# A gated cross-attention and spiking-FFN layer: attention's rows kept in PSUM, high halves read in place, and a new order on every engine

## What is computed

```python
def _mlstm_cell(q, k, v, igate_w, igate_b, fgate_w, fgate_b, ln_scale):
    ...
    log_f = jax.nn.log_sigmoid(fg)
    cs = jnp.cumsum(log_f, axis=1)
    ...
    log_D = log_fg_mat + ig[:, None, :]
    max_log_D = jnp.max(log_D, axis=-1, keepdims=True)
    D_mat = jnp.exp(log_D - max_log_D)
    qk = jnp.einsum('hsd,htd->hst', qh, kh) / np.sqrt(DH)
    C = qk * D_mat
    normalizer = jnp.maximum(jnp.abs(C.sum(axis=-1, keepdims=True)), jnp.exp(-max_log_D))
    h = jnp.einsum('hst,htd->hsd', C / (normalizer + EPS), vh)
    ...
    return (h - mu) / jnp.sqrt(var + LN_EPS) * ln_scale

def _L0_ffn_ref(x, W_fc, W_proj):
    h = jnp.square(jax.nn.relu(jnp.einsum('bsd,fd->bsf', x, W_fc)))
    y = jnp.einsum('bsf,df->bsd', h, W_proj)
    def step(mem, _):                      # 5 steps
        reset = spike_fn(mem - THRESHOLD)
        mem_new = BETA * mem + y - reset * THRESHOLD
        return (mem_new, spike_fn(mem_new - THRESHOLD))
    ...
    return jnp.sum(spks, axis=0) / NUM_STEPS

x = x + jnp.tanh(g_xattn[0]) * _L0_xattn_ref(_layernorm(x), ctx_1024, ctx_1024, ...)
x = x + jnp.tanh(g_ffn[0]) * _L0_ffn_ref(_layernorm(x), L0_ffn_W_fc, L0_ffn_W_proj)
```

## Time and profile before

| | us |
|---|---|
| time, median of 3 runs | 738.58 |
| lowest, highest | 737.99, 739.53 |
| the profiled execution's own time | 738.68 |
| its span | 736.9 |
| PE busy | 631.4 |
| PEld busy | 528.3 |
| DVE busy | 597.5 |
| ACT busy | 466.7 |
| POOL busy | 396.5 |

### The profile page before, as it was taken

How to read it: one execution, slowest core, us unless ns; L and a number is a source line. 1 busy time by engine, 2 the same in 40 slices (tenths; PEclk the granted TensorE clock), 3 DMA queues, 4 the chain that set the end, 5 groups by cost and what they waited for, 6 DMA issues and landing times. The chain is left out here.

```text
span 736.9 us, 17412 instructions
## 1 busy us (share of the span) xinstructions
PE 631.4 (86%) x6064; PEld 528.3 (72%) x6064; DVE 597.5 (81%) x1314; ACT 466.7 (63%) x1020; POOL 396.5 (54%) x427
## 2 busy tenths in 40 slices
PE   0254686889999989998999989998999999999985
PEld 0144675768787778877888778877887887787875
DVE  4577668889799979998799979997999889878543
ACT  4366665578577847676667747684778756764431
POOL 5346636656584656576466657575556645642000
PEclk9998789989999999999999999999999999999998
DMA  6946513396155724564266606672455444100000
GB/s 209 156 104 138 124 45 84 88 166 142 30 133 110 138 61 102 117 132 102 73 104 136 154 19 132 124 146 63 103 117 89 88 74 86 63 1 29 30 30 28
DMA packets 73174, 71.31 MB, mean 97 GB/s; under 512 B 8704, under 2 KB 68736, under 8 KB 73088
## 3 DMA queue, kind: packets, MB, share of 16 engines
q1 hardware_dynamic: 71968, 70.02, 44.8%
q10 hardware_dynamic: 1120, 0.18, 0.1%
HBM read 27.44 MB, written 8.39 MB: 49 GB/s over the span
## 5 line engine op out<-in xcount | busy, mean ns | idle before, releaser
L727 POOL TENSOR_TENSOR c_lo<-decay,c_hi 128x512 bf16<-128x512 f32 x128 | 156.6, 1229 | 103.4 <-ACT c_hi L720 103.4
L1029 PE MATMUL y_ps<-wpr,relu 128*128 128x256 f32 x680 | 167.5, 388 | 0.1
L1029 PEld LDWEIGHTS y_ps<-wpr,relu 128*128 128x128 f32 x680 | 125.9, 192 | 16.6 <-ACT relu L1015 0.6
L993 PE MATMUL z_ps<-x_hi,wfc_hi 128*128 128x512 f32 (+1 forms) x288 | 125.3, 435 | 5.4 <-ACT relu L1003 3.0
L703 ACT ACTIVATE decay<-arg_ps,lqk_col 128x512 f32<-128x512 f32 x128 | 87.3, 682 | 36.2 <-PE arg_ps L680 25.7
L993 PE MATMUL z_ps<-x_hi,wfc_lo 128*128 128x512 f32 (+1 forms) x288 | 107.3, 373 | 0.0
L993 PE MATMUL z_ps<-x_lo,wfc_hi 128*128 128x512 f32 (+1 forms) x288 | 106.9, 371 | 0.0
L711 DVE TENSOR_TENSOR decay<-qk_ps,decay 128x512 f32<-128x512 f32 x128 | 86.7, 677 | 17.9 <-PE qk_ps L692 11.8
L720 ACT ACTIVATE c_hi<-decay 128x512 bf16<-128x512 f32 x128 | 79.1, 625 | 22.6 <-DVE decay L711 22.5
L1003 ACT ACTIVATE relu<-z_ps 128x512 f32<-128x512 f32 (+1 forms) x96 | 52.3, 544 | 60.1 <-PE z_ps L993 59.5
L1029 PE MATMUL y_ps<-wpr,w_raw 128*128 128x256 f32 x344 | 84.2, 386 | 0.1
(11 more groups left out here) (136 smaller groups left out, 1632.8 us busy)
## 6 DMA issues: line engine op xcount, KB each, us to landing
v_in<-ctx_rows SPq DMA_DIRECT2D x32, 256.0 KB, 3.9
kT_in<-ctx_cols SPq DMA_DIRECT2D x32, 256.0 KB, 2.9
x_in<-x SPq DMA_DIRECT2D x32, 256.0 KB, 3.0
...
```

The lines of the kernel that those rows point to most:

```text
L727: e.tensor_tensor(c_lo[i % NCH][:, :], decay[i % NUN][:, :], c_hi[i % NCH][:, :], ALU.subtract).then_inc(sem("c_lo"), 1)
L993: ins = e.matmul(z_ps[:, tokens(q)], lhsT, rhs, start=(n == 0), stop=(n == len(terms) - 1))
L1029: ins = e.matmul(y_ps[:, t, :], relu[n % NRE][:, t * P:(t + 1) * P], wpr[:, j, :], start=(j == 0 and t % ST == 0), stop=(j == FT - 1), ski ...
```

## The change

1. c_hi, kw_hi and s_hi go. A new function top(tile) reads a float32 tile as bf16, every second element, which is its upper half (cut off, not rounded). c_lo_step, k_weigh_lo and state_lo subtract this; pv and state take it as the weights, inter as the moving data. ACT's c_hi_step, k_weigh_hi and state_hi don't exist any more. decay has six buffers for three and is held until pv has read it.
2. h_norm adds the late part into pv_ps in place and writes its result into pv_ps too (h_ps, the first 256 columns of the two banks); the denominators and the last product are one instruction for both tiles instead of two. The statistics read h_ps, x1_step's first step works in it and its second reads it. state(b) now waits for x1_done(b-1), since it writes the same banks.
3. The last spikes_step writes the count to y_ps, and out_step reads it there. y_step(q, 0) waits for out_done of the job before.
4. SQUARES_ON_POOL is empty: all squares are on ACT.
5. The fixed rows have tiles of their own, and the programs of all five engines and misc_order are written in a new order with a longer prologue (PE's body begins with y_step(2n-1, 3) instead of z_step(2n-1, 4)).

```diff
-SQUARES_ON_POOL = (3, 7)
+SQUARES_ON_POOL = ()
-    NX, NC, NQ, NK, NST, NV, NAM, NUN, NCH, NX1, NX2, NRE, NXL = 8, 2, 6, 4, 3, 2, 2, 3, 5, 3, 2, 6, 2
+    NX, NC, NQ, NK, NST, NV, NAM, NUN, NCH, NX1, NX2, NRE, NXL = 8, 2, 6, 4, 3, 2, 2, 6, 5, 3, 2, 6, 2
...
+        h_ps = pv_ps[:, :, 0:D]
+        def top(tile):
+            return tile.bitcast(bf16)[:, 1::2]
...
         def decay_exp(e, b, u):
-                e.wait_ge(sem("c_lo"), i - NUN + 1)
+                e.wait_ge(sem("pv"), (i - NUN) // UPH + 1)
...
-        def c_hi_step(e, b, u):
-            e.activation(c_hi[i % NCH][:, :], decay[i % NUN][:, :], ACT.Copy).then_inc(sem("c_hi"), 1)
         def c_lo_step(e, b, u):
-            e.wait_ge(sem("c_hi"), i + 1)
-            e.tensor_tensor(c_lo[i % NCH][:, :], decay[i % NUN][:, :], c_hi[i % NCH][:, :], ALU.subtract).then_inc(sem("c_lo"), 1)
+            e.wait_ge(sem("cmul"), i + 1)
+            if i - NCH >= 0:
+                e.wait_ge(sem("pv"), (i - NCH) // UPH + 1)
+            c = decay[i % NUN][:, :]
+            e.tensor_tensor(c_lo[i % NCH][:, :], c, top(c), ALU.subtract).then_inc(sem("c_lo"), 1)
         def pv(e, b, half):
-                    hi, lo = c_hi[slot][:, cols], c_lo[slot][:, cols]
+                    hi, lo = top(decay[i % NUN][:, cols]), c_lo[i % NCH][:, cols]
...
         def state(e, b):
-                e.wait_ge(sem("h_norm"), b)
+                e.wait_ge(sem("x1_done"), b)
-                hi, lo = kw_hi[:, c * P:(c + 1) * P], kw_lo[:, c * P:(c + 1) * P]
+                hi, lo = top(kw[:, c * P:(c + 1) * P]), kw_lo[:, c * P:(c + 1) * P]
...
         def h_norm(e, b):
-            link(e, "vector", e.tensor_tensor(late, pv_heads[:, 1, :, :], late, ALU.add))
-            row_sum, least = (pv_heads[:, 0, :, DH], late[:, :, DH]), floor[g % 3][:, :, row:row + NH]
-            for t in range(ST):
-                ins = e.scalar_tensor_tensor(denom[:, t, :], row_sum[t], -1.0, least[:, t, :], ALU.mult, ALU.max)
-            link(e, "vector", ins)
-            for t in range(ST):
-                ins = e.tensor_tensor(denom[:, t, :], denom[:, t, :], row_sum[t], ALU.max)
-            link(e, "vector", ins)
+            link(e, "vector", e.tensor_tensor(pv_heads[:, 1, :, :], pv_heads[:, 1, :, :], late, ALU.add))
+            row_sum, least = pv_heads[:, :, :, DH], floor[g % 3][:, 0:ST, row:row + NH]
+            link(e, "vector", e.scalar_tensor_tensor(denom[:, :, :], row_sum, -1.0, least, ALU.mult, ALU.max))
+            link(e, "vector", e.tensor_tensor(denom[:, :, :], denom[:, :, :], row_sum, ALU.max))
             link(e, "vector", e.tensor_scalar(denom[:, :, :], denom[:, :, :], EPS, None, ALU.add))
             link(e, "vector", e.reciprocal(rdenom[:, :, :], denom[:, :, :]))
-            for t, src in enumerate((pv_heads[:, 0, :, 0:DH], late[:, :, 0:DH])):
-                ins = e.tensor_tensor(heads[:, t, :, :], src, rdenom[:, t, :].unsqueeze(2).broadcast_to([P, NH, DH]), ALU.mult)
-            ins.then_inc(sem("h_norm"), 1)
+            e.tensor_tensor(h_ps.rearrange("p t (h d) -> p t h d", d=DH), pv_heads[:, :, :, 0:DH],
+                            rdenom[:, :, :].unsqueeze(3).broadcast_to([P, ST, NH, DH]), ALU.mult).then_inc(sem("h_norm"), 1)
...
         def x1_step(e, b):
-                ins = e.scalar_tensor_tensor(h_rows[:, t, :], h_rows[:, t, :], mv2[:, t, 0:1], scale_row[:, :],
+                ins = e.scalar_tensor_tensor(h_ps[:, t, :], h_ps[:, t, :], mv2[:, t, 0:1], scale_row[:, :],
                                              ALU.subtract, ALU.mult)
...
-                ins = e.scalar_tensor_tensor(dst[:, t, :], h_rows[:, t, :], rstd2[:, t:t + 1], x_in[b % NX][:, t, :],
+                ins = e.scalar_tensor_tensor(dst[:, t, :], h_ps[:, t, :], rstd2[:, t:t + 1], x_in[b % NX][:, t, :],
                                              ALU.mult, ALU.add)
...
         def y_step(e, q, j):
-                    e.wait_ge(sem("spikes"), STEPS * (job_before(q) + 1))
+                    e.wait_ge(sem("out_done"), job_before(q) + 1)
...
         def spikes_step(e, q, n):
-                ins = e.scalar_tensor_tensor(count, y, THETA[n], count, ALU.is_gt, ALU.add)
+                total = y if n == STEPS - 1 else count
+                ins = e.scalar_tensor_tensor(total, y, THETA[n], count, ALU.is_gt, ALU.add)
         def out_step(e, q):
-            e.scalar_tensor_tensor(out_sb[:, tiles, :], spikes[:, tiles, :], rate_g[:, :], x1[p % NX1][:, tiles, :],
+            e.scalar_tensor_tensor(out_sb[:, tiles, :], y_ps[:, tiles, :], rate_g[:, :], x1[p % NX1][:, tiles, :],
                                    ALU.mult, ALU.add).then_inc(sem("out_done"), 1)
...
         def sync_program(e):
-            load_values(e, 0)
-            load_k(e, 0)
             load_x(e, 0)
             load_x(e, 1)
+            load_values(e, 0)
...
         def scalar_program(e):
             setup_load_small(e)
+            setup_tanh(e)
             ln1_rstd(e, 0)
-            setup_tanh(e)
```

More of the change, by code:

```diff
@@ L810, in state_own, with state_lo @@
                             ALU.mult).then_inc(sem("state_own"), 1)
-        def state_hi(e, b):
+        def state_lo(e, b):
             if not 0 <= b < B:
@@ new lines, in vector_program @@
+            ln3_stats(e, 3)
+            q_lo(e, 9)
+            cmul(e, 5, 0)
+            cmul(e, 5, 1)
+            h_norm(e, 4)
+            ln2_stats(e, 4)
+            cmul(e, 5, 2)
+            x1_step(e, 4)
+            ln3_offset(e, 3)
+            spikes_step(e, 0, 3)
+            x2_lo_step(e, 2)
+            cmul(e, 5, 3)
+            state_own(e, 5)
+            ln1_stats(e, 11)
+            cmul(e, 6, 0)
+            ln1_offset(e, 5)
+            ln3_stats(e, 4)
+            x2_lo_step(e, 3)
@@ new lines, in tensor_program @@
+            y_step(e, 1, 0)
+            qk(e, 4, 2)
+            arg(e, 4, 3)
+            z_step(e, 1, 4)
+            qk(e, 4, 3)
+            y_step(e, 1, 1)
+            qk(e, 5, 0)
+            pv(e, 4, 0)
+            arg(e, 5, 0)
+            gate_products(e, 8)
+            q_T(e, 9)
+            y_step(e, 1, 2)
+            arg(e, 5, 1)
+            pv(e, 4, 1)
+            inter(e, 4)
+            qk(e, 5, 1)
+            gate_products(e, 9)
+            arg(e, 5, 2)
+            z_step(e, 1, 5)
```

1132 lines of the change are left out of this document (583 added, 549 removed), and 6 rows, old and new, of the table order.

## The result

The changed kernel takes **689.15 us** (median; 687.64 to 691.28) beside 738.62 us for the kernel before: ratio 0.933, 95% interval 0.930 to 0.936. That is 49.5 us less, where 42.7 were forecast; it lies within the range. The profiled execution took 687.64 us.

The account below looks back on a forecast made before the run. PE and DVE, both near 90% busy and waiting for each other through single buffers, were taken to set the 80 us period. With a period of 75: 738.7 - 27.5 (body) - 13 (start) - 2 (end) = 696 us, range 676 to 731.

Parts of the forecast that it names:

- DVE's prices: DVE per repeated period: instructions with one PSUM source get cheaper, 10.9 us less, busy time from 72.2 to about 61.
- row 863's PSUM source is the nearest: DVE: why the whole 10.9 us was taken, though no row shows a PSUM destination's price; line 863 from pv_ps takes 424 ns.
- POOL need not gain: POOL per period: by the row alone no gain from less contention with DVE; only four squares go, 5 of 49 us.
- PE's floor: PE per period: counted by starts, 71 of 80 us of work, leaving 9 us of slack; the floor for the new period.
- Start: First 160 us: earlier table loads and x give 4 us, lighter batches 9; together 13, bounds 4 to 22.
- end: From 600 us on: one period's gain on part of it, less the later y_steps; 2 us, bounds -1 to 5.
- The order holds the period: Rival for the repeated period: hand-written in-order queues keep 78 to 79 us despite lighter work; 715 to 731 us, chance 0.14.
- Strided loads: Rival on PE: pv and state weights using every second element cost 4.8 us a period; 734 us, band 731 to 745, chance 0.07.
- The wait for x1_done shows: Rival at state(b): part of 13 us per period of new waiting is uncovered; e.g. 754 us, over 745, chance 0.07.
- if PE waits for x at the state: Sign on PE at the state: the prediction named such a wait as showing it wrong; no size given.
- a chain of 10 us in a batch of 18: Cover for the x1_done wait: state through x1 adds up to about 10 us, while a batch has 18 us.
- Doesn't do what it says: Rival on DVE: x1_step's lines cost 645 and 930 in PSUM too; about 718 us, within the order rival's band, no separate chance.

Follow-up runs that it names:

- a_no_vlo: The changed kernel without the 512 matmuls of pv that multiply c's high half by v's low half: 684.0 us.
- a_contig_imm: The changed kernel with packed bf16 tiles as weights in pv and state, and constants for rate_g in out_step and the mean in x1_step: 686.8 us.
- a_dve_old: The changed kernel with parts 2 and 3 undone (attention's rows and the count in SBUF), the state still waiting for x1_done: 765.7 us.
- a_dve_old_hn: The changed kernel with parts 2 and 3 undone and the state waiting for h_norm of the batch before instead of x1_done: 736.9 us.
- b_start: The kernel before with only the start changed: x loaded first, tanh_g and both table loads ahead of ACT's wait for the statistics: 735.1 us.
- b_light: The kernel before, in its own order, without line 893's two instructions per batch and with four thresholds counted instead of five: 712.8 us.
- a_dve_load: The changed kernel with an extra DVE statistics instruction of 448 fixed columns behind every cmul from the third batch on: 722.4 us.
- a_four: The changed kernel with one of the five counting instructions of each job left out: 687.0 us.

## Why the prediction held, step by step

**The direction and the mechanism** held. The repeated period became PE's (99.5% busy), from one that PE and DVE set by waiting for each other; that PE binds it is shown in part (a_no_vlo: about half of what PE loses is had, the rest is taken by the next hand-overs).

**DVE's prices.** Forecast 424 ns for x1_step and 1215 for out_step, 10.9 us per period; measured 480 to 484, 1275, and 71.9 to 62.3, 9.6 us. The step that was mis-sized is "row 863's PSUM source is the nearest": line 863 takes no number per partition, and that is the missing 57 ns (a_contig_imm). A destination in PSUM costs nothing, as taken: counts into y_ps take 1223 ns, into SBUF 1218. Of the 14 us by which DVE's busy time of 524 us exceeds the forecast 510, this is some 8 (128 x 57 ns and 18 x 60). Two causes differ from what the forecast took. out_step's price fell mainly by its place: 1337 ns with its SBUF sources in the new order (a_dve_old), 1275 with one in PSUM. And the norms' small offsets (line 358, then 361), which read two SBUF tiles and which I had left alone, fell from 410 to 221 ns, 9 us in the run.

**POOL and ACT.** ACT went from 56.4 to 48.3 per period, within its bounds (400 us in all, where I named 385). POOL lost 9.9, not 5 (49.1 to 39.2): its c_lo went from 1229 to 1042 ns. In a_dve_old_hn, with the new c_lo but rows and count in SBUF, it takes 1108, so 66 ns are DVE's doing. The other 121 belong to c_lo's new operands: where no DVE instruction with all its sources in SBUF runs beside it, c_lo takes 1162 ns in before and 1040 in after (medians of 42 and 74 instances). That POOL need not gain was the wrong choice of my two.

**PE's floor.** I counted 71 us; it is near 74. The term that failed most is the z_step: 1.38 us of the earlier trace rows holds when it runs alone, but behind another operation its first matmul is followed after 0.33 us, not 0.23:

```profile
295.67 0.50 PE L971 MATMUL z_ps<-x_hi,wfc_hi 128*128 128x512 f32 x1
296.00 0.40 PE L971 MATMUL z_ps<-x_lo,wfc_hi 128*128 128x512 f32 x1
296.24 0.39 PE L971 MATMUL z_ps<-x_hi,wfc_lo 128*128 128x512 f32 x1
```

Summed over a period of after by starts, z_ps takes 24.4 us where I had 22.1, y_ps 27.0 for 27.7, qk 3.4 for 3.0, state and inter 3.3 for 2.6, and gate products with the gates' transposes 3.2 for 2.9. So PE's slack in before was some 6.5 us per period, not 9. The forecast of 75 came out near 74.1 because I stood off a floor that was itself too low: two errors that cancel, and in that the number was lucky.

**The period of before** was 80.4, not 80: every second one has a stretch of 3.4 us at the lower level (0.98 on average, 81.0 us), after a wait of PE of 2.1 us at qk for cmul. The other two periods have that wait too, without a fall; after's periods have neither. The body gave 32.8 us for the forecast's 27.5, 6.3 per period where I had 5.

**Start** 14.1 for 13, **end** 4.1 for 2, both within their bounds. Of the start 3 to 4 is the head (b_start). Another piece I had no term for may be the clock: granted 0.89 in the first 160 us of before, 0.97 in after. a_contig_imm has after's order and 0.89 in its profiled execution, and its job 1 is counted at 148.85, 3.7 us later than in after; a cause by the clock isn't shown by this pair alone. The rest, 6 to 7 us or more, is left for the lighter batches and wasn't measured apart.

**The rivals.** "The order holds the period" fell by b_light. "Strided loads" fell by a_contig_imm. "The wait for x1_done shows" didn't come true in after (4.2 us in the whole run, in three waits that end at 101.5, 113.2 and 207.1, ahead of the four periods; by the letter, the sign "if PE waits for x at the state" was met), but it is real: with rows in SBUF it costs 29 us. My cover for it, a chain of 10 us in a batch of 18, was the wrong reckoning: it would have covered a_dve_old too. Two things were seen to cover it: the chain h_norm to x1 became shorter by the very edit that needs the wait (9.8 to 7.8 us), and DVE's queue became lighter (with the short chain and a full DVE, a_dve_load, PE waits 5.9 us for x again). They weren't parted further. "Doesn't do what it says" fell by the rows of lines 871 and 876.

**What I had not seen** is how strongly the parts need each other. By b_light (26.2 us for 61) a microsecond of DVE is worth 0.43 in the old order, which makes some 31 of 49.5 us out of the 73.6 us that DVE lost (an estimate); by a_dve_load (33.3 for 74) it is worth 0.45 in the new one, and by a_four 0.1 beyond it. How the other 18 us divide between the start (3 to 4), the copies that ACT lost and the order is not settled: copies and order were not taken out of the change one by one. Nor had I seen the clock in this: where PE's waits grow long, rows at the lower level follow in the body, and they add to what the wait costs.
